# Loading the codes of `down` as f16 by GpSimd's DMAs instead of through the staging ring and ScalarE

## What is computed

```python
# x: (1024, 512) tokens, normalised first; gate_t, up_t: (1792, 512) int32 codes in {-1, 0, 1}
# down_t: (512, 1792) int32 codes; gate_s, up_s: (1792,), down_s: (512,) f32 scales
gate_out = x_flat @ (gate_t * gate_s[:, None]).T
up_out   = x_flat @ (up_t * up_s[:, None]).T
hidden   = silu(gate_out) * up_out
out_flat = hidden @ (down_t * down_s[:, None]).T
```

## Time and profile before

| | |
|---|---|
| median of three runs | 340.98 us |
| lowest and highest run | 337.39 and 341.88 us |
| span of the profiled execution | 338.4 us |
| TensorE busy | 304.7 us (90% of the span) |
| VectorE busy | 219.2 us (65%) |
| GpSimd busy | 150.9 us (45%) |
| ScalarE busy | 122.1 us (36%) |
| DMA queues | 22.68 MB in 12120 packets; all from SP, none from GpSimd |

### The profile page before, as it was taken

How to read it: one execution, slowest core, us unless ns; L and a number is a source line. 1 busy time by engine, 2 the same in 40 slices (tenths; PEclk the granted TensorE clock), 3 DMA queues, 4 the chain that set the end, 5 groups by cost and what they waited for, 6 DMA issues and landing times.

```text
span 338.4 us, 4458 instructions
## 1 busy us (share of the span) xinstructions
PE 304.7 (90%) x1524; PEld 189.8 (56%) x1524; DVE 219.2 (65%) x454; ACT 122.1 (36%) x195; POOL 150.9 (45%) x161
## 2 busy tenths in 40 slices
PE   1886678989899999999899898997899999999995
PEld 0753334736446554646456364453356888888784
DVE  4597899798955678575856756658677752333313
ACT  1662363452653103061542516203012573126520
POOL 3577153947433220234524444426025797018930
PEclk9999797999999999999999999999799999999999
DMA  7863335264520103101100111110001000030003
GB/s 232 336 176 138 105 112 157 93 189 108 171 99 27 31 2 86 39 14 31 31 25 1 31 33 31 31 33 0 1 0 65 1 0 2 2 122 2 1 0 124
DMA packets 12120, 22.68 MB, mean 67 GB/s; under 512 B 1345, under 2 KB 1730, under 8 KB 12098
## 3 DMA queue, kind: packets, MB, share of 16 engines
q1 hardware_dynamic: 12098, 22.40, 21.1%
HBM read 20.30 MB, written 2.10 MB: 66 GB/s over the span
## 4 chain that ended last, share of the span: by engine, by line
PE 70%; DVE 15%; POOL 7%; issue 4%; ACT 2%; DMA 1%; SPq 0%; DVEq 0%; ACTq 0%; POOLq 0%
PE bank L717 10%; PE bank L623 9%; PE bank L624 9%; PE bank L592 8%; PE bank L590 8%; PE bank L591 8%; PE bank L677 5%; PE bank L584 2%; PE bank L669 2%; DVE lno L955 2%; PE bank L656 2%; PE bank L650 2%; PE bank L668 2%; DVE uscan L973 2%; POOL root L1078 2%
## 5 line engine op out<-in xcount | busy, mean ns | idle before, releaser
L1136 POOL TENSOR_TENSOR hidl<-hid,hidh 128x512 f16<-128x512 f32 x28 | 34.1, 1218 | 69.3 <-ACT hidh L783 69.3
L623 PE MATMUL bank<-xh,gatew 128*128 128x512 f16 (+1 forms) x124 | 44.7, 371 | 1.7 <-DVE xl L912 1.4
L623 PE MATMUL bank<-xh,upw 128*128 128x512 f16 (+1 forms) x124 | 45.0, 373 | 0.3 <-ACT upw L809 0.3
L624 PE MATMUL bank<-xl,upw 128*128 128x512 f16 (+1 forms) x124 | 44.9, 372 | 0.0
L624 PE MATMUL bank<-xl,gatew 128*128 128x512 f16 (+1 forms) x124 | 44.5, 369 | 0.0
L1078 POOL TENSOR_TENSOR root<-var,powers 128x4 f32<-128x4 f32 (+1 forms) x25 | 24.6, 983 | 43.5 <-DVE var L944 34.7
L717 PE MATMUL bank<-downw,hidh 128*128 128x512 f16 x112 | 43.0, 384 | 0.0
L717 PE MATMUL bank<-downw,hidl 128*128 128x512 f16 x112 | 42.8, 382 | 0.0
L845 ACT ACTIVATE silu<-bank,early 128x512 f32<-128x512 f32 x28 | 19.2, 687 | 60.7 <-PE bank L624 60.7
L1142 POOL TENSOR_TENSOR actl<-hid,acth 128x512 fp32r<-128x512 f32 (+1 forms) x22 | 28.3, 1298 | 22.6 <-ACT acth L790 22.4
L941 DVE BATCH_NORM_STATS2 st<-bank 128x6 f32<-128x64 f32 x72 | 11.4, 219 | 25.6 <-PE bank L677 14.8
(11 more groups left out here) (144 smaller groups left out, 650.8 us busy)
## 6 DMA issues: line engine op xcount, KB each, us to landing
stage<-in_gate SPq DMA_DIRECT2D x14, 256.0 KB, 4.1
stage<-in_up SPq DMA_DIRECT2D x14, 256.0 KB, 2.7
stage<-in_down SPq DMA_DIRECT2D x14, 256.0 KB, 3.0
X<-in_x SPq DMA_DIRECT2D x8, 256.0 KB, 5.5
out_x<-X SPq DMA_DIRECT2D x8, 256.0 KB, 2.0
stage<-in_v SPq DMA_DIRECT2D x6, 256.0 KB, 2.7
stage<-in_mask SPq DMA_DIRECT2D x4, 256.0 KB, 2.7
stage<-in_weight SPq DMA_DIRECT2D x4, 256.0 KB, 2.7
```

What stands on the lines that cost most here:

```text
L623: pe.matmul(bank_of(key)[:, c], w, xh[b][:, k, c], start=(k == 0), stop=False)
L624: mm = pe.matmul(bank_of(key)[:, c], w, xl[b][:, k, c], start=False, stop=(k == KT - 1))
L1136: pool.tensor_tensor(hidl[:, n % FT, :], hid[:, n % UNITS, :], hidh[:, n % FT, :], ALU.subtract).then_inc(hid_lo, 1)
```

## The change

Each pair of tiles of `down` (512 KB of int32 in HBM) is loaded by one DMA that GpSimd issues, seven in all. The destination is `downw` itself, whose elements are f16, so the conversion is made in the DMA. The load of tiles `f` and `f` + 1 stands where the cast of tile `f` stood, for even `f`. The 14 tiles of `down` leave the staging ring (and SP's list) and ScalarE. TensorE waits for all seven loads in front of the first matmul of `down`.

```diff
@@ build_order
-        after[up_at(0, f)].append(("cast", "down", f))
+        if f % DOWN_LOAD == 0:
+            after[up_at(0, f)].append(("load", "down", f))
@@ constants
+DOWN_LOAD = 2
@@ cast_by_act
-    return kind == "down" or i == 0 or (kind == "up" and 1 < i < ACT_UPS)
+    return i == 0 or (kind == "up" and 1 < i < ACT_UPS)
@@ two_layers
-    ternary = {e: [c for c in casts if c[0] in ("gate", "up", "down") and (cast_by_act(*c) == (e == "act"))]
+    ternary = {e: [c for c in casts if c[0] in ("gate", "up") and (cast_by_act(*c) == (e == "act"))]
                for e in ("act", "dve")}
...
+        down_in = sem("down_in")
@@ TensorE, step down
                         if t == 0:
-                            for by in codes_ready:
-                                pe.wait_ge(codes_ready[by], len(ternary[by]))
+                            pe.wait_ge(down_in, 16 * (FT // DOWN_LOAD))
@@ GpSimd
+                elif kind == "load":
+                    f = step[2]
+                    pool.dma_start(codes["down"][:, f:f + DOWN_LOAD, :],
+                                   down[f:f + DOWN_LOAD].rearrange("f p d -> p f d")).then_inc(down_in, 16)
```

## The result

| | before | changed |
|---|---|---|
| median of 20 runs | 340.95 us | 343.88 us |
| lowest and highest | 336.06 and 342.85 us | 340.05 and 346.05 us |
| span of the profiled execution | 338.4 us | 341.1 us |

The ratio is 1.0112, with a 95% interval of 1.0073 to 1.0150. It compares the means of the fast runs alone, 16 of the changed kernel (343.2 us) and 12 of the kernel before (339.4 us), while the medians in the table are of all 20 and give 1.0086. The change makes the kernel slower by about 1%: 2.9 us by the medians, 3.8 us by those means, 2.7 us by the spans of one execution each.

What follows compares the result with a forecast made beforehand. Before `down`, the stretch was taken as bound first by VectorE, later by TensorE. 0 + 0 + 0.4 + 2.8 + 1.7 = +4.9 us on the 338.4 us span, plus 2.6 us to the median, gave 345.9 us, range 340.0 to 350.5.

Steps and rivals of the forecast that it cites:

- ScalarE's 8.7 us at nothing: Taking the 14 casts of `down`, 8.7 us, off ScalarE was valued at 0.
- The third rival: ScalarE's 1.1 us wait for a `down` load goes, TensorE's idle before 51.9 us shrinks: faster, 338.7 us; chance 0.06.
- The ring and SP at nothing: Taking 14 issues off SP and 14 slot turns off the staging ring was valued at 0.
- D: Price of one DMA issue on GpSimd: taken as 1.2 us, bounds 0.33 and 1.77 us.
- The roots behind tiles 8 and 12: GpSimd's `root` at 81.69 and 101.22 us each start D late, hidden up to D = 2.4 and 3.1 us.
- VectorE held up, +0.4: The load of tile 2, at 42.5 us, lengthens a VectorE cast: +0.4 us, ends 0 and 3.4 us.
- The last load: Load of tiles 12 and 13 lands at 106.1 us; TensorE stalls 2.8 us at the start of `down`, ends 1.1 and 6.6.
- The 3.2 us that the prediction set beside it as an estimate: The Trainium skill's estimate for a 512 KB GpSimd DMA; with it the stall would be 2.2 us.
- the signs that the prediction named: First `down` wait 2 to 4 us, clock below 1, seven 1.2 us issues, ScalarE 8.7 us less busy, late `root` at 81.7.
- The clock, +1.7: Behind the stall at `down` the granted clock drops as it did from 52 to 57 us: +1.7 us.
- the first rival: Last load all but hidden: stall 1.1 us, no clock drop, nothing on VectorE, 342.1 us; chance 0.22.
- The sum: 0 (ScalarE) + 0 (ring) + 0.4 (VectorE) + 2.8 (stall) + 1.7 (clock) = +4.9 us.

Runs made afterwards that it cites:

- e4_act_back: e1_early with 14 casts of 512 columns that nobody reads given back to ScalarE; ratio to the kernel before 1.0041, median 341.47 us.
- b3_before_allact: The kernel before with all casts of gate and up except those of tile 1 on ScalarE; ratio 0.9861, median 335.54 us.
- e6_mid: The changed kernel with the seven loads moved: three behind up of tile 6, two behind tile 10, two behind tile 11; ratio to the kernel before 1.0039.
- e1_early: The changed kernel with each load two tiles earlier in the order; ratio to the kernel before 1.0014, median 341.61 us.
- e2_waits: The changed kernel with a semaphore and a TensorE wait for each load instead of one for all; ratio to the kernel before 1.0036, median 341.64 us.
- e7_fourteen_mid: The changed kernel with 14 loads of one tile at the places of e6_mid; ratio to the kernel before 1.0028.
- e5_fourteen: e1_early with 14 loads of one tile instead of seven of two; ratio to the kernel before 1.0212.

## Why the prediction was right, and where its sizes were off

**ScalarE's 8.7 us at nothing: right.** e4_act_back gives them back without a loss that can be seen, and b3_before_allact adds 20 casts more and gets faster. The third rival (faster, since ScalarE's wait for a load of `down` goes) did not come: the wait for `ymini` ahead of 52 us is there as before, 3.3 us against 3.0.

**The ring and SP at nothing: right as far as it goes.** No TensorE wait on codes changed. It was not tried by itself.

**D, the issue on GpSimd: too high.** 0.77 us against the 1.2 taken, within the bounds of 0.33 and 1.77. The roots behind tiles 8 and 12 were late by 0.6 us and hidden: each starts 1.86 us behind the start of its `hidl` instead of 1.26, and `lno` waited for a root no longer than before (2.2 us over the whole span in both).

**VectorE held up, +0.4: not to be seen.** The cast at 40.3 us, the first of W1, took 1.38 us against 0.41 in the kernel before, but 1.1 us of that pass beside the `hidl` and only 0.3 beside the load of tile 2. In the kernel before it was the `rot` ahead of the cast that met the `hidl` (1.59 us, here 0.69), so the two took 2.00 us together before and 2.07 after the change. VectorE's busy time is 218.9 against 219.2 us. In e6_mid, without loads in that stretch, TensorE's wait for `ymini` is 2.6 instead of 3.3 us, but the kernel is no faster than e1_early.

**The last load: the right step, 1.4 us too long.** The stall was there, at the place and for the cause named, with 1.4 instead of 2.8 us. The step that failed is "I take 3.8 and put D ahead of it: 1.2 + 3.8 = 5.0 us". The 3.8 us of the earlier trace rows are counted from the issue, so they hold an issue already; D was counted twice. Measured from the start of GpSimd's issue the last load took 3.8 us, as the plain one of 512 KB. The 3.2 us that the prediction set beside it as an estimate would have been 0.6 us short. The other 0.2 us is that the load went out at 100.7, 2.4 instead of 2.2 us ahead of the end of `w2`. Of the signs that the prediction named, the place and the cause of the wait, the low clock and the hidden root are there; a wait of 2 to 4 us, issues of 1.2 us and 8.7 us less of busy ScalarE are not (1.4, 0.77 and 7.5).

**The clock, +1.7: right in kind, measured 1.4.** Here the forecast was right by its own stall and would have been wrong for the real one: it said that the clock falls behind 2.8 us and, in the first rival, that it stays up behind about 1.1. It fell behind 1.4 us. That the sizes 1.7 and 1.4 agree so well owes something to luck. The row on which that rival rested, 1.5 us of idle time at 68.4 with a clock of 1.00 behind it, did not carry over.

**The sum.** Predicted +4.9, measured +2.9 by the medians: 1.4 less stall, 0.3 less clock, 0.4 less on VectorE, 2.1 in all. The traces give 1.4 + 1.4 = 2.8 us for stall and clock, but the edits that remove both take back only some 2.3 us of the median (343.9 to 341.6, on another chip). What the runs leave open is about 0.6 us: the kernels that load by GpSimd and have no stall (e1_early, e2_waits, e4_act_back, e6_mid, e7_fourteen_mid) have medians 0.4 to 1.3 us above the kernel before. Three of the five intervals hold 1.000 and two (e2_waits, e4_act_back) just miss it, but all five ratios lie on the same side. The number of issues and their place between 20 and 68 us don't explain it. The list of runs narrows it down. The runs with a mean granted clock of at most 0.979 have medians of 341.8 to 342.0 us in these five kernels and 341.7 to 342.0 us in the three series of the kernel before. But the kernel before had a higher clock in 44 of its 81 runs, these five in 23 of 60. So what is left lies mostly in how often the clock was low; why that should differ, the runs don't tell.

## What to carry to other kernels

When a load moves to another engine's queue, ask what it then stands behind: the last of the seven was tied to the `hidl` of tile 12 and so to TensorE's own progress, 2.4 us ahead of its use, where the loads of the ring had run far ahead. A single wait for all parts in front of the first use makes the latest part the price of all; a wait for each part, or the loads two tiles earlier, took it away here. And a relief is worth what its engine sets: 8.7 us off ScalarE gave nothing that can be seen, 13.3 us off VectorE gave 1.4%, by one line. Before two spans are compared, look at where each lost time to the clock: the same kernel's traces differ there by 1.7 us at a time.

## What the runs showed of the hardware that was not expected

- A DMA of GpSimd that turns 512 KB of int32 into 256 KB of f16 costs GpSimd 0.72 to 0.94 us. It landed 3.6 to 6.1 us after its issue where the loads stood apart, and up to 8.3 us after it where three were issued in a row (e6_mid). With half the size it is 0.54 to 0.77 us, and 2.9 to 3.9 us or, several in a row (e7_fourteen_mid), up to 5.7 us. The conversion made the last load no slower than the one plain 512 KB load on a quiet queue, 3.8 us.
- An idle time of TensorE of 1.4 us was followed by 3.0 us at a mean granted clock of 0.53, one of 4.1 us by about the same loss, and with six matmuls in the gap the clock was 1.00 (one trace). An idle time of 1.5 us at 68.4 in the kernel before had no such effect, and one of 1.6 us in the second layer had it in nine traces and not in five; the runs don't tell why.
- A cast on VectorE that takes 0.43 us by itself lasted 5.16 us beside a row of GpSimd instructions without a pause (e5_fourteen); beside the same additions it took 1.47 us in e1_early.
